# Four output buffers in place of two for the first expert layer of a two-layer decoder kernel

## The chip, the core and the metric

The kernel runs on one core of a Trainium2 chip. The core has a matrix engine (PE, with its weight loads as PEld), a vector engine (DVE), a scalar engine (ACT), a general engine (POOL), a sequencer that mostly issues DMAs (SP), and 16 DMA engines. Each engine works through its own instruction list in order, and they meet by semaphores. The metric is the device time of one launch in microseconds (us); lower is better.

## The reference

2048 tokens of 256 numbers go through two decoder layers. What matters here is the mixture of experts that closes the first layer:

```
scores = softmax(xt @ Wg.T)                      # 16 experts in 4 groups
gidx   = top_k(max of each group, 2)             # 2 groups kept
topi   = top_k(scores in the kept groups, 4)     # 4 experts for each token
h      = silu(xt @ W1[e]) * (xt @ W3[e])         # 176 wide, for each expert e
y      = sum over the 4 of score * (h @ W2[e])
z      = silu(xt @ Ws1.T) * (xt @ Ws3.T) @ Ws2.T # the shared experts
x      = layernorm(x + y + z)
```

Ahead of it stand a quadratic linear attention and a cross attention, behind it the second layer: a causal attention, a cross attention and a second mixture (8 experts, 2 for each token, 1024 wide).

## The kernel before

The stage in question is `moe0`. Tokens are sorted by expert into 79 slots of 128 rows (`NT`); a slot belongs to one expert. POOL scatters the token rows from SBUF into the table `xs` in HBM (L1614, an indirect DMA for each token tile and choice, 64 in all). The slots are then worked off in an order that a small table gives: SP (and ACT for the first seven) loads slot j's rows into `XG` once all the token tiles that the slot needs are in place. The result of a slot goes to the table `ys` in HBM, and POOL gathers it from there for each token tile (L1434, four indirect DMAs a tile), scales it by the gates and adds it to `X`.

The work on slot j is a software pipeline over four engines (`tile_pipeline`, L1411: a hardware loop with four slots a pass, the last seven slots written out). In step j:

- PE turns slot j+3 (`rows`, L1812), multiplies slot j+2 by W1 and W3 (`gate_up`, L1820), turns the product of slot j+1 (L1826), and multiplies slot j by W2 into the PSUM bank `BY[j % 2]` (L1840, L1842);
- ACT copies the turned rows j+3 (`XGT`, L1677), computes silu for slot j+2 (L1681), copies the turned product j+1 (L1685), and then issues the store of output j (`store`, L1688 to L1691), for which it waits until DVE has copied that output;
- DVE multiplies the gate of slot j+2 (L1756), and then copies output j from PSUM to `Y[j % 2]` in SBUF (L1764). This copy waits for `y_full` (PE is done with slot j) and for `stored[j % 2]` (the store of slot j-2, which read the same half of `Y`, has landed). It increments `y_used`.

So a copy to `Y` implies that the store of two slots before has landed. That is how POOL knows what it may gather: `ready_on_dve` (L1217) computes for each token tile t the place of the last slot that holds one of its rows, plus 1, plus `ahead` = 2, and POOL waits for `y_used` to reach it (`may_fetch`, L1627). At the end SP waits for all stores and adds 2 to `y_used` (L1580 to L1582), so that the last tiles can be released.

POOL's work in this stage is one chain: scatter, then for 12 of the 16 token tiles wait, gather, scale, add (`add_rows`, L1444). Two points in it are waited for by DVE: after tile 3 a semaphore `whole`, for which DVE waits behind slot 55 (moments of the first four tiles, L1482), and behind tile 9 the reciprocal roots of these moments (L1491, L1492), for which DVE waits behind slot 67 before it normalizes these tiles (L1497). Both sit in DVE's list between two hardware loops, ahead of the next slot's work.

PE ends the stage with ten matmuls whose results nobody reads (L152). A barrier of all engines follows, and then the second layer.

The second mixture, `moe1` (L2840 on), has the same pattern with its own `Y` of two buffers, ACT as the copying engine (L2994, L2995) and two semaphores `stored` of its own.

Of the kernel before, what the change touches and what calls it, by code (L numbers as in the profile page):

```python
# [14 lines left out]
BATCH, SEQ, DIM = 32, 64, 256  # L15
# [15 lines left out]
EPS_LN, EPS_RMS = 1e-5, 1e-6  # L31
NEG = -1.0e30
HS, SC = SHARED * I0, 3


REGION = TILES
# [1463 lines left out]
def moe0(nc, es, io, fx):  # L1500
# [8 lines left out]
    with ExitStack() as mem:  # L1509
# [3 lines left out]
        def sem(name):  # L1513
            return es.enter_context(nc.semaphore("m0_" + name))
# [7 lines left out]
        Z = sb("Z", [P, TILES, DIM])  # L1522
        XG, XGT = GS[:].rearrange("p a (b d) -> p (a b) d", d=DIM), sb("XGT", [P, 2, KC * P])
        SG, H, HT = sb("SG", [P, 2, I0]), sb("H", [P, 2, I0]), fx.HT
        Y = US[:, 0, :].rearrange("p (b d) -> p b d", d=DIM)
        BT, BH, BU, BY = fx.PJ, fx.SB[0:2], fx.SB[2:4], fx.OB
        ld_sh, ld_w, padded = fx.ld_sh, sem("ld_w"), fx.padded
        sh_full, sh_used, sh_h = sem("sh_full"), sem("sh_used"), sem("sh_h")
# [5 lines left out]
        u_full, gate, h_done = sem("u_full"), sem("gate"), sem("h_done")  # L1534
        ht_full, ht_used = sem("ht_full"), sem("ht_used")
        y_full, y_used = sem("y_full"), sem("y_used")
        stored = [sem(f"stored{b}") for b in range(2)]
        due, gathered = sem("due"), [sem(f"gathered{b}") for b in range(2)]

        with nc.Block() as block:  # L1540
            @block.sync
            def _(sp):
                for b in range(2):
                    sp.sem_inc(stored[b], 16)
                sp.wait_ge(fx.slots_zeroed, 64)
                for m in range(KC):
                    sp.dma_start(W13[:, m], io["w13"][m, :, 0:E0, :]).then_inc(ld_w, 16)
                sp.dma_start(W2A[:], io["w2"][0:P, 0:E0, :]).then_inc(ld_w, 16)
                sp.dma_start(W2B[0:KI], io["w2"][P:I0, 0:E0, :]).then_inc(ld_w, 16)
                sp.dma_start(W2B[KI:P], fx.zeros[KI:P].unsqueeze(1).broadcast_to([P - KI, E0, DIM])).then_inc(ld_w, 16)  # L1550
                sp.wait_ge(r.placed, 2)

                def load(j, b, checked=None):
                    if checked is not None:
                        need = sp.value_load(r.tneed[0:1, bass.ds(checked, 1)], min_val=1, max_val=TILES)
                    s = sp.value_load(r.tslot[0:1, bass.ds(j, 1)], min_val=0, max_val=NT - 1)
                    sp.wait_ge(t_full, j + 1)
                    if checked is not None:
                        sp.wait_ge(in_place, need)
                    sp.dma_start(XG[:, b, :].unsqueeze(1), slots[:, bass.ds(s, 1), :]).then_inc(ld_x[b], 16)  # L1560

                def weights():
                    fx.l1.load_weights(sp, io)

                load(FIRST, FIRST % 4, FIRST)
                with sp.Fori(0, CHECKED // 4) as i:
                    for b in range(4):
                        load(i * 4 + (FIRST + 1 + b), b, i * 4 + (FIRST + 4) if b == 0 else None)
                sp.wait_ge(in_place, TILES)
                done = FIRST + 1 + CHECKED  # L1570
                for upto, visit in ((48, weights), (NT - (NT - done) % 4, None)):
                    with sp.Fori(0, (upto - done) // 4) as i:
                        for b in range(4):
                            load(i * 4 + (done + b), b)
                    if visit:
                        visit()
                    done = upto
                for j in range(NT - (NT - FIRST - 1) % 4, NT):
                    load(j, j % 4)
                for b in range(2):  # L1580
                    sp.wait_ge(stored[b], 16 + 16 * ((NT + 1 - b) // 2))
                sp.sem_inc(y_used, 2)  # L1582

            @block.gpsimd
            def _(pool):
# [39 lines left out]
                own = fx.pool_steps  # L1625

                def may_fetch(t):  # L1627
                    pool.wait_ge(y_used, pool.value_load(r.ready[0:1, t:t + 1], min_val=3, max_val=NT + 2))
                    pool.sem_inc(due, 1)

                def fetch(t, k):
# [17 lines left out]
            def _(act):  # L1649
# [38 lines left out]
                def store(j, b):  # L1688
                    s = act.value_load(r.tslot[0:1, bass.ds(j, 1)], min_val=0, max_val=NT - 1)
                    act.wait_ge(y_used, j + 1)  # L1690
                    act.dma_start(rows_out[:, bass.ds(s, 1), :], Y[:, b % 2, :].unsqueeze(1)).then_inc(stored[b % 2], 16)  # L1691

                def step(j, b, ahead):
                    if follows(ahead, 3):
# [35 lines left out]
            def _(dve):  # L1730
# [10 lines left out]
                def gated(n):  # L1741
# [5 lines left out]

                r.order_on_dve(nc, dve, fx.slot_no[:], fx.ident[:], fx.tile_row[:], BU[0], BU[1], gated,
                               ((POOL_GATES, POOL_GATES + 1), (POOL_GATES + 2,)))
                r.ready_on_dve(nc, dve, fx.ident[:], BU[0], BU[1], 2, gated,  # L1750
                               ((POOL_GATES + 3,), (POOL_GATES + 4,)))
                gated(POOL_GATES + 5)

# [5 lines left out]
                def step(j, b, ahead):  # L1759
                    if follows(ahead, 2):  # L1760
                        product(j + 2, b + 2)
                    dve.wait_ge(y_full, j + 1)
                    dve.wait_ge(stored[b % 2], 8 * (j + (2 - b % 2)))
                    nc.vector.tensor_copy(Y[:, b % 2, :], BY[b % 2][:, 0:DIM]).then_inc(y_used, 1)  # L1764

                product(0, 0)
                product(1, 1)
# [1047 lines left out]
def moe1(nc, es, io, fx):  # L2815
# [7 lines left out]
    with ExitStack() as mem:  # L2823
# [3 lines left out]
        def sem(name):  # L2827
            return es.enter_context(nc.semaphore("m1_" + name))
# [24 lines left out]
        t_full, t_used = sem("t_full"), sem("t_used")  # L2853
        u_full, h_gelu = sem("u_full"), sem("h_gelu")
        y_full, y_used, finished = sem("y_full"), sem("y_used"), sem("finished")
        stored = [sem(f"stored{b}") for b in range(2)]
        due, gathered = sem("due"), [sem(f"gathered{i}") for i in range(AHEAD)]
        moments, root = sem("moments"), sem("root")
        normed, written = sem("normed"), sem("written")
# [5 lines left out]
        with nc.Block() as block:  # L2865
            @block.sync
            def _(sp):
# [29 lines left out]
                def step(j, b, ahead, checked=False):  # L2897
                    if follows(ahead, 6):
                        load(j + 6, (b + 2) % 4, checked)
                    if follows(ahead, WB):  # L2900
                        load_w1(j + WB, b, 2 * j + 4)
                    s = slot(j)
                    sp.wait_ge(stored[(b + 1) % 2], 8 * j + (16 if b % 2 == 0 else 24))
                    sp.sem_inc(finished, 1)  # L2904
                    sp.wait_ge(y_used, j + 1)
                    sp.dma_start(rows_out[:, bass.ds(s, 1), :], Y[:, b % 2, :].unsqueeze(1)).then_inc(stored[b % 2], 16)

# [7 lines left out]
                sp.wait_ge(in_place, TILES)  # L2915
                tile_pipeline(sp, step, NS, done=CHECKED)
                for b in range(2):
                    sp.wait_ge(stored[b], 16 + 16 * ((NS + 1 - b) // 2))
                sp.sem_inc(finished, 1)
                sp.wait_ge(written, 16 * POOL_WRITES)  # L2920
                sp.wait_ge(ld_s, 48 + 16 * (PAIRS - POOL_WRITES))
# [52 lines left out]
            def _(act):  # L2974
# [13 lines left out]
                def step(j, b, ahead):  # L2988
                    if follows(ahead, 2):
                        rows(j + 2, b)  # L2990
                    if follows(ahead, 1):
                        gelu(j + 1, b + 1)
                    act.wait_ge(y_full, j + 1)
                    act.wait_ge(stored[b % 2], 8 * (j + (2 - b % 2)))  # L2994
                    nc.scalar.activation(Y[:, b % 2, :], BY[b % 2][:, 0:DIM], ACT.Copy).then_inc(y_used, 1)  # L2995

                act.sem_inc(t_used, FIRST)
# [192 lines left out]
def decoder(nc, io):  # L3190
    es = ExitStack()
    with es:
        fx = Fixed()

        def sb(name, shape):
# [25 lines left out]
        fx.slots_zeroed = es.enter_context(nc.semaphore("slots_zeroed"))  # L3221
        fx.LG1 = sb("LG1", [P, TILES, E1])
        fx.early_table = es.enter_context(nc.sbuf_tensor("early_table", [P, 2, EARLY_TILES], I32))
        fx.early_placed, fx.early_sent, fx.in_place = (es.enter_context(nc.semaphore(n)) for n in (
            "early_placed", "early_sent", "in_place"))
        early = es.enter_context(ExitStack())
# [103 lines left out]
```

## Time and profile before

| | us |
|---|---|
| median of three runs | 1193.8 |
| the three runs | 1188.15, 1193.8, 1194.08 |
| the profiled execution | 1193.7 |
| its span, first to last instruction | 1191.9 |
| share of the span: PE, DVE, ACT, POOL | 91%, 42%, 42%, 37% |
| granted PE clock, mean | 0.964 |

The profiled execution lies 0.1 us from the median. 1.8 us of its time lie outside the span. All positions in the text are microseconds from the start of the span. The stage `moe0` runs its expert loop from about 384 to 616 us; the second mixture's loop takes the last 300 us. "m_US" in rows of `moe0` is the tile that `Y` is a part of, "m_GS" the one that `XG` is a part of, "bank" is PSUM, "inputs" is the tile that holds `HT`. PE works in float32 here, with several passes for one product, so a row of L1820 counts x4 for one slot.

### The profile page before, as it was taken

The numbers are of one execution on the slowest core, as the hardware profiler recorded it, in microseconds if no ns is written. First come the engines' busy times: TensorE is split into PE (matmuls) and PEld (weight loads), VectorE is DVE, ScalarE is ACT, GpSimd is POOL, SyncE is SP. The second block draws the span as 40 slices with busy tenths as digits, with TensorE's granted clock in tenths as the row PEclk, the third lists the DMA queues.
The fourth block names the chain that finished last, engine by engine and source line by source line (L and its number), as shares of the span: only waits on it lengthen the run. The fifth ranks groups of instructions, "written<-read, shape, count | busy, mean of one in ns | idle before, by whom it ended". The sixth has DMA issues, their size and how long they took to land. (4 is left out here: it accounts for less than half of the span.)

```text
span 1191.9 us, 29025 instructions
## 1 busy us (share of the span) xinstructions
PE 1087.6 (91%) x10260; PEld 838.5 (70%) x10261; DVE 496.3 (42%) x1340; ACT 504.1 (42%) x1306; POOL 439.9 (37%) x563
## 2 busy tenths in 40 slices
PE   8889989988898679999988999998789999999998
PEld 4466666655455347777756777786579899899997
DVE  2366665545571113333325666767443800000323
ACT  2444544444432123333334666575344333333333
POOL 2022131311248852777654666332524000200434
PEclk9999999999999669999999999999789999999999
DMA  6199478021283334565536111000157555555673
GB/s 202 45 311 362 161 237 268 21 81 55 118 258 118 129 113 126 154 191 150 144 120 284 37 37 53 22 19 3 56 194 237 187 175 177 174 175 174 194 240 107
DMA packets 119339, 176.09 MB, mean 148 GB/s; under 512 B 17440, under 2 KB 96912, under 8 KB 117776
## 3 DMA queue, kind: packets, MB, share of 16 engines
q1 hardware_dynamic: 94448, 135.55, 34.9%
q0 software_dynamic: 9696, 26.75, 6.9%
q10 hardware_dynamic: 15088, 12.28, 3.1%
q8 instruction: 77, 1.26, 0.4%
q14 instruction: 30, 0.25, 0.1%
HBM read 105.07 MB, written 68.16 MB: 145 GB/s over the span
## 5 line engine op out<-in xcount | busy, mean ns | idle before, releaser
L3149 PE MATMUL bank<-w,m_HT 128*128 x624 | 141.0, 379 | 0.0
L2984 ACT ACTIVATE m_HT<-bank,m_b 128x128 f32<-128x128 f32 x312 | 88.9, 370 | 90.2 <-PE bank L3135 74.2
L3149 PEld LDWEIGHTS bank<-w,m_HT 128*128 128x128 f32 x624 | 115.7, 190 | 14.1
L1820 PE MATMUL bank<-m_W,m_XGT 128*128 x316 | 114.0, 485 | 9.0 <-ACT m_XGT L1677 6.8
L1434 POOL DMA_INDIRECT GA<-ys,r_pos x64 | 64.7, 1010 | 62.9 <-DVE m_US L1764 43.0
L1677 ACT ACTIVATE m_XGT<-bank 128x256 f32<-128x256 f32 x79 | 30.3, 384 | 129.2 <-DVE m_US L1764 80.1
L1756 DVE TENSOR_TENSOR m_H<-bank,m_SG 128x176 f32<-128x176 f32 x79 | 26.9, 341 | 135.7 <-ACT m_SG L1681 96.9
L2948 POOL DMA_INDIRECT m_GA<-ys,r_pos x32 | 31.6, 986 | 133.6 <-SPq L2904 124.9
L3135 PE MATMUL bank<-m_XGT,m_w1a 128*128 128x128 f32 x640 | 77.3, 279 | 2.6 <-issue 1.8
L1820 PEld LDWEIGHTS bank<-m_W,m_XGT 128*128 128x128 f32 x316 | 56.6, 199 | 30.2 <-issue 14.3
L3135 PEld LDWEIGHTS bank<-m_XGT,m_w1a 128*128 128x128 f32 x640 | 75.0, 195 | 3.5 <-issue 2.3
L1614 POOL DMA_INDIRECT xs<-X,r_pos x64 | 63.2, 987 | 27.8 <-issue 14.6
L3135 PE MATMUL bank<-m_XGT,m_w 128*128 128x128 f32 x608 | 71.0, 275 | 0.0
L3135 PEld LDWEIGHTS bank<-m_XGT,m_w 128*128 128x128 f32 x608 | 69.5, 192 | 0.1
L405 POOL TENSOR_SCALAR l_rs<-l_mv 128x2 f32<-128x2 f32 x16 | 3.6, 225 | 158.2 <-DVE l_mv L669 157.9
L1764 DVE COPY m_US<-bank 128x256 f32<-128x256 f32 x79 | 33.5, 424 | 48.8 <-PE bank L1842 32.5
L1840 PE MATMUL bank<-m_W2A,inputs 128*128 x158 | 50.9, 405 | 2.9 <-issue 1.8
L1842 PE MATMUL bank<-m_W2B,inputs 128*128 x158 | 49.3, 395 | 0.0
L2995 ACT ACTIVATE m_Y<-bank 128x256 f32<-128x256 f32 x39 | 15.1, 386 | 80.2 <-PE bank L3149 75.5
L64 PE MATMUL bank<-XT,inputs 128*128 128x512 f32 x96 | 43.2, 596 | 2.7 <-ACT raw L481 1.3
L3057 DVE TENSOR_TENSOR X<-bank,X 128x512 f32<-128x512 f32 x8 | 5.5, 692 | 94.0 <-PE bank L3111 94.0
L2553 PE MATMUL bank<-l_VX,l_WX 128*64 128x54 f32 x1024 | 37.8, 234 | 7.5 <-issue 5.6
(475 smaller groups left out, 2301.3 us busy)
## 6 DMA issues: line engine op xcount, KB each, us to landing
m_w1a<-in_m_w SPq DMA_DIRECT2D x20, 1024.0 KB
m_w<-in_m_w SPq DMA_DIRECT2D x19, 1024.0 KB
xs<-zeros SPq DMA_DIRECT2D x1, 10112.0 KB, 34.2
ys<-zeros SPq DMA_DIRECT2D x1, 10112.0 KB, 34.6
ys<-m_US ACTq DMA_DIRECT2D x79, 128.0 KB
m_GS<-xs SPq DMA_DIRECT2D x72, 128.0 KB
w<-in_m_w SPq DMA_DIRECT2D x8, 1024.0 KB, 11.9
xs<-zeros SPq DMA_DIRECT2D x1, 6400.0 KB, 23.7
```

The lines of the kernel that those rows point to most:

```text
L64: last = nc.tensor.matmul(dst, stills[i], movings[i], start=i == 0, stop=i == n - 1)
L1434: pool.indirect_dma_start(out=fx.GA[:, t % 2 * (t < EARLY), k, :], out_offset=None, in_=fx.ys, in_offset=bass.IndirectOffsetOnAxis(ap=fx.p ...
L1614: pool.indirect_dma_start(out=fx.xs, out_offset=bass.IndirectOffsetOnAxis(ap=r.pos[:, t, k:k + 1], axis=0), in_=fx.X[:, t, :], in_offset=N ...
L1764: nc.vector.tensor_copy(Y[:, b % 2, :], BY[b % 2][:, 0:DIM]).then_inc(y_used, 1)
L1820: last = nc.tensor.matmul(BU[b % 2][:, 0:IW], XGT[:, b % 2, m * P:(m + 1) * P], W13[:, m, bass.ds(e, 1), :], start=m == 0, stop=m == KC - 1)
L1840: nc.tensor.matmul(BY[b % 2][:, 0:DIM], HT[:, b % 2, 0, :], W2A[:, bass.ds(e, 1), :], start=True, stop=False)
L1842: nc.tensor.matmul(BY[b % 2][:, 0:DIM], HT[:, b % 2, 1, :], W2B[:, bass.ds(e, 1), :], start=False, stop=True).then_inc(y_full, 1)
L2553: last = nc.tensor.matmul(repeated(OB[t][a * SEQ:(a + 1) * SEQ, n * 18:(n + 3) * 18], 18), WX[:, t, r, m, c], over_again(VX[:, j % 2, t, h ...
L2948: pool.indirect_dma_start(out=GA[:, t, k, :], out_offset=None, in_=fx.ys, in_offset=bass.IndirectOffsetOnAxis(ap=fx.pos1[:, t, k:k + 1], a ...
L2984: last = nc.scalar.activation(HT[:, b % 2, at, :], BU[i][:, c * P:(c + 1) * P], ACT.Gelu, bias=b1[:, b % WB, at:at + 1])
L3135: last = nc.tensor.matmul(BU[i][:, c * P:(c + 1) * P], w1[b][:, m, lo:lo + P], XGT[:, b % 2, m * P:(m + 1) * P], start=m == 0, stop=m == K ...
L3149: last = nc.tensor.matmul(BY[b % 2][:, 0:DIM], HT[:, b % 2, c, :], w2[:, bass.ds(e, 1), c, :], start=c == 0, stop=c == CH - 1)
```

## The change

`Y` gets four buffers: the whole tile `US` in place of its first half. Each buffer has its own store semaphore (`stored` with four entries, allocated for the whole kernel instead of for the stage). A copy to `Y[j % 4]` now waits for the store of slot j-4. What POOL may gather is released accordingly: `ahead` is 4, and the end adds 4 to `y_used`. The second mixture goes on counting on the first two of the same semaphores, so that its thresholds have an offset (`stores_of_first`).

```diff
+YB = 4
-        Y = US[:, 0, :].rearrange("p (b d) -> p b d", d=DIM)
+        Y = US[:].rearrange("p i (b d) -> p (i b) d", d=DIM)
-        stored = [sem(f"stored{b}") for b in range(2)]
+        stored = fx.stored
@@ moe0, SP
-                for b in range(2):
+                for b in range(YB):
                     sp.sem_inc(stored[b], 16)
...
-                for b in range(2):
-                    sp.wait_ge(stored[b], 16 + 16 * ((NT + 1 - b) // 2))
-                sp.sem_inc(y_used, 2)
+                for b in range(YB):
+                    sp.wait_ge(stored[b], fx.stores_of_first[b])
+                sp.sem_inc(y_used, YB)
@@ moe0, POOL: may_fetch
-                    pool.wait_ge(y_used, pool.value_load(r.ready[0:1, t:t + 1], min_val=3, max_val=NT + 2))
+                    pool.wait_ge(y_used, pool.value_load(r.ready[0:1, t:t + 1], min_val=YB + 1, max_val=NT + YB))
@@ moe0, ACT: store
-                    act.dma_start(rows_out[:, bass.ds(s, 1), :], Y[:, b % 2, :].unsqueeze(1)).then_inc(stored[b % 2], 16)
+                    act.dma_start(rows_out[:, bass.ds(s, 1), :], Y[:, b, :].unsqueeze(1)).then_inc(stored[b], 16)
@@ moe0, DVE
-                r.ready_on_dve(nc, dve, fx.ident[:], BU[0], BU[1], 2, gated,
+                r.ready_on_dve(nc, dve, fx.ident[:], BU[0], BU[1], YB, gated,
...
-                    dve.wait_ge(stored[b % 2], 8 * (j + (2 - b % 2)))
-                    nc.vector.tensor_copy(Y[:, b % 2, :], BY[b % 2][:, 0:DIM]).then_inc(y_used, 1)
+                    dve.wait_ge(stored[b], 4 * j + (16 - 4 * b))
+                    nc.vector.tensor_copy(Y[:, b, :], BY[b % 2][:, 0:DIM]).then_inc(y_used, 1)
@@ moe1, SP and ACT: the same waits, with what moe0 has counted added
-                    sp.wait_ge(stored[(b + 1) % 2], 8 * j + (16 if b % 2 == 0 else 24))
+                    sp.wait_ge(stored[(b + 1) % 2], 8 * j + (16 if b % 2 == 0 else 24) + earlier[(b + 1) % 2])
...
-                    act.wait_ge(stored[b % 2], 8 * (j + (2 - b % 2)))
+                    act.wait_ge(stored[b % 2], 8 * j + (8 * (2 - b % 2) + earlier[b % 2]))
@@ whole kernel
+        fx.stored = [es.enter_context(nc.semaphore(f"stored{b}")) for b in range(YB)]
+        fx.stores_of_first = [16 + 16 * ((fx.NS0 - b + YB - 1) // YB) for b in range(YB)]
```

No engine's arithmetic changes and nothing of it changes place. What changes in the lists is how a copy takes its two waits. On DVE, slots 1, 2 and 3 of a pass of the hardware loop in `moe0` (bank 7 and bank 6 hold the outputs, `m0_US` is `Y`, ISA stands for an instruction that only waits) are, before:

```order
L1756 TENSOR_TENSOR m0_H<-bank5,m0_SG 128x176 [waits m0_gate]
L1764 COPY m0_US<-bank7 128x256 [waits m0_stored1,m0_y_full]
L1755 REGISTER_ALU
L1756 TENSOR_TENSOR m0_H<-bank4,m0_SG 128x176 [waits m0_gate]
L1763 REGISTER_ALU [waits m0_y_full]
L1764 COPY m0_US<-bank6 128x256 [waits m0_stored0]
L1755 REGISTER_ALU
L1756 TENSOR_TENSOR m0_H<-bank5,m0_SG 128x176 [waits m0_gate]
L1764 COPY m0_US<-bank7 128x256 [waits m0_stored1,m0_y_full]
```

and now:

```order
L1757 TENSOR_TENSOR m0_H<-bank5,m0_SG 128x176 [waits m0_gate]
L1763 REGISTER_ALU
L1764 ISA [waits m0_y_full]
L1765 COPY m0_US<-bank7 128x256 [waits stored1]
L1756 REGISTER_ALU
L1757 TENSOR_TENSOR m0_H<-bank4,m0_SG 128x176 [waits m0_gate]
L1764 ISA [waits m0_y_full]
L1765 COPY m0_US<-bank6 128x256 [waits stored2]
L1756 REGISTER_ALU
L1757 TENSOR_TENSOR m0_H<-bank5,m0_SG 128x176 [waits m0_gate]
L1764 ISA [waits m0_y_full]
L1765 COPY m0_US<-bank7 128x256 [waits stored3]
```

Each copy now waits only for its own buffer's semaphore, and the wait for `y_full` stands in an instruction ahead of it; the copies of odd slots used to carry both waits themselves. A pass of four slots has three more sequencer instructions in each of DVE's two hardware loops; the slots written out behind them wait as before.

On ACT, in the second mixture's loop, the copy of an odd slot's output (`m1_Y` from bank 7) was:

```order
L2981 REGISTER_ALU
L2984 ACTIVATE m1_HT<-bank3,m1_b1 128x128 [waits m1_u_full]
L2984 ACTIVATE m1_HT<-bank3,m1_b1 128x128 x3
L2995 ACTIVATE m1_Y<-bank7 128x256 [waits m1_stored1,m1_y_full]
L2976 REGISTER_ALU
```

and is now:

```order
L2982 REGISTER_ALU
L2985 ACTIVATE m1_HT<-bank3,m1_b1 128x128 [waits m1_u_full]
L2985 ACTIVATE m1_HT<-bank3,m1_b1 128x128 x3
L2995 ISA [waits m1_y_full]
L2996 ACTIVATE m1_Y<-bank7 128x256 [waits stored1]
L2977 REGISTER_ALU
```

Here too the odd copy's wait for `m1_y_full` has moved into an instruction of its own.

## Rows read from the trace of the kernel before

**Rows 1.** Page, part 2: the clock of PE in 40 slices of 29.8 us, in tenths.

```profile
PEclk9999999999999669999999999999789999999999
```

**Rows 2.** Waits, 385 to 625 us: engine, its work <- releaser: us in total, times, longest.

```profile
POOL GA L1434 <- DVE m_US L1764: 43.0, 6, 27.3
DVE m_US L1764 <- PE bank L1842: 32.5, 56, 3.9
...
DVE m_US L1764 <- DMA ys<-m_US: 1.4, 1, 1.4
```

**Rows 3.** Timeline, one steady step: start, us, engine, line, op [idle before <-releaser].

```profile
447.63 0.42 DVE L1764 COPY m_US<-bank 128x256 f32<-128x256 f32 x1 [0.48 <-PE bank L1842]
...
448.21 0.34 ACTq L1691 DMA_DIRECT2D ys<-m_US  x1
...
448.67 0.38 ACT L1677 ACTIVATE m_XGT<-bank 128x256 f32<-128x256 f32 x1 [1.57 <-DVE m_US L1764]
...
450.03 0.42 DVE L1764 COPY m_US<-bank 128x256 f32<-128x256 f32 x1 [0.39 <-PE bank L1842]
450.05 0.46 PE L1820 MATMUL bank<-m_W,m_XGT 128*128 x1
```

**Rows 4.** Timeline, the stretch in which POOL still scatters.

```profile
388.33 0.59 PE L1842 MATMUL bank<-m_W2B,inputs 128*128 x2
...
391.84 0.42 DVE L1764 COPY m_US<-bank 128x256 f32<-128x256 f32 x1 [3.86 <-PE bank L1842]
...
399.77 0.42 DVE L1764 COPY m_US<-bank 128x256 f32<-128x256 f32 x1 [3.65 <-remote]
...
407.13 0.42 DVE L1764 COPY m_US<-bank 128x256 f32<-128x256 f32 x1 [2.33 <-remote]
```

**Rows 5.** Timeline, around the copy that waits for a store.

```profile
523.07 0.34 ACTq L1691 DMA_DIRECT2D ys<-m_US  x1
...
527.38 1.35 PE L1820 MATMUL bank<-m_W,m_XGT 128*128 x4
...
528.38 0.42 DVE L1764 COPY m_US<-bank 128x256 f32<-128x256 f32 x1 [1.40 <-DMA ys<-m_US]
...
529.94 1.45 PE L1820 MATMUL bank<-m_W,m_XGT 128*128 x4
...
532.70 1.45 PE L1820 MATMUL bank<-m_W,m_XGT 128*128 x4
```

**Rows 6.** Source line 1764 (the copy of an output), 391 to 498 and 391 to 503 us.

```profile
L1764 DVE COPY m_US<-bank x31: 424/425/426, 391.8 to 497.6; 128x256 f32<-128x256 f32 x31
...
L1764 DVE COPY m_US<-bank x33: 424/425/426, 391.8 to 502.6; 128x256 f32<-128x256 f32 x33
```

**Rows 7.** Timeline of POOL: gathers of tiles 3 and 11, and its last work here.

```profile
498.83 1.03 POOL L1434 DMA_INDIRECT GA<-ys,r_pos  x1 [5.00 <-DVE m_US L1764]
...
586.18 1.05 POOL L1492 TENSOR_TENSOR l_rs<-l_rs,neghalf 128x4 f32<-128x4 f32 x1
593.75 1.10 POOL L1434 DMA_INDIRECT GA<-ys,r_pos  x1 [6.53 <-DVE m_US L1764]
...
607.69 0.72 POOL L1454 TENSOR_TENSOR X<-X,GA 128x256 f32<-128x256 f32 x1
```

**Rows 8.** Timeline, DVE at the moments; DVE and PE at the normalization.

```profile
560.50 1.39 DVE L1482 BATCH_NORM_STATS2 l_st<-X 128x6 f32<-128x256 f32 x4
...
590.36 1.37 DVE L1497 TENSOR_SCALAR X<-X,l_mv,l_rs 128x256 f32<-128x256 f32 x4
...
591.92 0.34 DVE L1756 TENSOR_TENSOR m_H<-bank,m_SG 128x176 f32<-128x176 f32 x1 [0.19 <-ACT m_SG L1681]
...
593.71 0.27 PE L1826 MATMUL bank<-ident,m_H 128*128 128x128 f32 x1
...
595.01 1.35 PE L1820 MATMUL bank<-m_W,m_XGT 128*128 x4
```

**Rows 9.** Timeline, first work of POOL behind the stage.

```profile
619.52 1.91 POOL L2030 MEMSET l_VS<- 128x2176 f32 x1 [11.10 <-POOLq L1540]
```

More of the change, by code:

```diff
@@ L2855, in moe1 @@
         y_full, y_used, finished = sem("y_full"), sem("y_used"), sem("finished")
-        stored = [sem(f"stored{b}") for b in range(2)]
+        stored, earlier = fx.stored, fx.stores_of_first
         due, gathered = sem("due"), [sem(f"gathered{i}") for i in range(AHEAD)]
@@ L2917, in _ @@
                 for b in range(2):
-                    sp.wait_ge(stored[b], 16 + 16 * ((NS + 1 - b) // 2))
+                    sp.wait_ge(stored[b], earlier[b] + 16 + 16 * ((NS + 1 - b) // 2))
                 sp.sem_inc(finished, 1)
```

## The prediction

> **What bounds the kernel now.** I read first the waits of the stage that the change touches, because a double buffer is worth something only if somebody waits for it. In 385 to 625 us DVE waited once for a store, 1.4 us in all; behind PE it waited 56 times for 32.5 us [rows 2]. POOL waited 43.0 us for DVE's copies, that is for the release of the gathers [rows 2]. Then I read one steady step in the timeline. PE is the engine with no gap: from the 31st to the 33rd copy 5.0 us pass, 2.5 us a slot [rows 6], and at full clock in all slices there but two [rows 1]. The reader is to see in rows 3 how little of the copy's chain matters: copy at 447.63, store issued at 448.21, ACT's next rows at 448.67 to 449.05, and PE needs these rows at 450.05. So about 1.0 us of slack lies between DVE's copy and PE. A store has from its issue (0.58 us after its copy starts) to the copy two slots later, 5.0 - 0.6 = 4.4 us, to land, and in the steady step nobody waits for it.
>
> Two stretches are different. At 391 to 438 us, where the clock falls to half [rows 1], a slot takes 7 to 8 us: copies at 391.84, 399.77, 407.13 [rows 4]. And around 528 us one copy waits for a store [rows 5].
>
> **The change part by part.** The sum is made against the profiled execution: 1191.9 us span, 1193.7 us with what lies around it, 0.1 under the median.
>
> *The waits that go.* The copy at 528.38 waited 1.40 us, against 0.4 to 0.5 in a steady step, so it came 0.9 to 1.0 us late. It waited for the store issued at 523.07, which took some 5.3 us. PE felt little: its next products follow 2.56 and 2.76 us apart (527.38, 529.94, 532.70) in place of 2.5 [rows 5], 0.3 us in all. With four buffers the store has 9.4 us, and the wait is gone. Gain 0.3 us; its ends are 0 and the whole 1.4 us of wait.
>
> The Trainium skill ("DMA: Bandwidth & Descriptors", on the fixed cost of a DMA) puts about 2 us on every DMA, mostly the receipt of the write, and adds bytes over 436 GB/s. By that a 128 KB store is an estimated 2.3 us, two buffers with 4.4 us never wait, and the gain would be 0. The row at 528.38 disagrees with that for one store of 79; the same section of the Trainium skill also allows a "surprisingly long delay" for writes to HBM, which is this case.
>
> *The slow stretch, 391 to 438 us.* If its copies waited for stores, this would be the big term. I read that they don't. Copies 0 and 1 wait for no store, as their semaphores start at 16. Yet copy 0 starts 2.9 us after PE is done with its slot (388.92), and copy 1 comes 7.9 us after copy 0 with an idle time that ends on "remote", not on a DMA [rows 4]. Copy 2 needs the store of slot 0, issued near 392.4, and starts at 407.13, 14.7 us later; no store that the trace blames took over 5.3. So the term is 0.
>
> *The released gathers.* A copy now implies that the store of four slots before has landed, so POOL waits for two more copies. Tile 3's gathers were released by the 31st copy (the last one before 498.83 [rows 6, 7]) and now by the 33rd: 502.6 - 497.6 = 5.0 us later. Of POOL's six waits for DVE, 43.0 us in all, three are long: 27.3 for the first tile, 5.0 for tile 3 and 6.5 for tile 11 [rows 2, 7]. The others share 4.2 us, so tiles 4 to 10 follow POOL's own chain and all move by 5.0 us, and with them the roots behind tile 9: they end at 586.18 + 1.05 = 587.2 us, now 592.2. The moments have cover: tile 11 takes POOL 608.4 - 593.8 = 14.6 us from its first gather to its last addition; even at twice that, tile 3, started at 503.8, is added up by 533, and DVE wants it at 560.50 [rows 7, 8]. Cost 0.
>
> DVE reaches the normalization at 590.36 and needs those roots [rows 8]. Before, they were 3.1 us early; now they are 1.9 us late, and this is a new wait. Queued behind it on DVE are four normalizations (1.37 us), the gate product for PE's next turn, and the copy that lets ACT issue a store and then fetch rows. The product moves from 591.92 to 593.6 and ends at 593.9; PE wanted it at 593.71 [rows 8], so PE loses 0.3 us. The copy starts at 593.95, ACT's rows end 1.04 + 0.38 us behind a copy's start [rows 3], at 595.4, and PE starts on them at about 595.5 instead of 595.01 [rows 8]: 0.5 us lost in all, these 0.3 included. After that the slack of 1.0 us takes the rest. Ends: 0, and the whole 1.9 us.
>
> This stall is tied to POOL's clock, which hangs on the 33rd copy, and that lies ahead of the 0.3 us won at 528. Won time makes DVE arrive sooner and wait longer. So behind 595 us the 0.3 is swallowed and the stage stands at +0.5, not +0.2. I take +0.5.
>
> POOL's last work moves from 608.4 to 613.4, or by the release of tile 11 two copies later than 593.75 to the same. POOL's next work is at 619.52 [rows 7, 9]. 6.1 us of cover hide it; beyond that each us would cost one. The final wait for four semaphores instead of two waits for the same last store: 0.
>
> *The waits' new form.* An odd slot's copy starts 0.39 us, an even one's 0.48 us behind the product before it [rows 3]; now all have the even form, 0.09 us more for every second slot. In steady steps the 1.0 us of slack hides it. In the slow stretch copy, store and rows follow on each other, and three odd copies add 0.3 us (ends 0 and 0.3). In the second mixture ACT's odd copy gets the same 0.1 us. PE's chain there waits for no copy of an output, so it costs 0; without that cover, 19 odd slots would be 2 us.
>
> Sum: +0.5 + 0.3 = +0.8 us: span 1192.7, time 1194.5 us.
>
> **The rivals.** What can be told from no change here is about 0.5%, 6 us, so nearly everything above is "the same".
>
> *Faster: the stretch at 391 us is a wait for stores after all.* For it: it is where DMAs of POOL's scatter are in flight, and a copy's two waits can't be told apart if one is unrecorded. Against it: copies 0 and 1, as above [rows 4]. Then about six slots fall from 7.4 to 2.5 us: 6 x 4.9 = 29 us, 1165 us. If only one or two slots are freed, 5 to 10 us, 1184 to 1189.
>
> *Slower: the stretch at 391 us holds more slots.* Place: the loop of copy, store, rows, product and copy, which there runs once in 7.4 us. The new instruction ahead of an odd copy lies on it. If it makes the loop miss the end of the stretch by a slot, that slot costs 4.9 us more; from two slots on (9.8 us, 1204 us) it is over 0.5%. For it: the stretch is sensitive to something that no row names. Against it: 0.3 us in 46 is little.
>
> *Slower: code loading in DVE's loop.* Its two loops run 17 passes and get longer by three instructions. If a pass had to load its code again, it would stall as long as the worst idle times there, 3.9 us [rows 4], of which 1.0 us is covered: 17 x 2.9 = 49 us, 1243 us. No steady step shows such a stall [rows 3]. The Trainium skill ("Runtime: NRT & Kernel Launch", on instruction fetch) says that a taken branch out of the window of two pages forces a fetch; a loop of some 20 instructions would leave that window in no pass.
>
> *The change does nothing.* The released gathers are not the last thing POOL waits for, or the root is in time: then 1193.7 less 0.3, and the reader sees no idle time ahead of L1497's normalizations.
>
> **How the numbers follow.** Small terms only, within 0.5%: 0.81, the "does nothing" case included. Stretch freed: 0.08, of it most over 0.5%. Stretch longer: 0.06. Code loading: 0.02. Other shifts of an execution, such as the runs' own 1188 to 1194: 0.03, both ways. So faster by over 0.5% 0.09, the same 0.82, slower 0.09. Time 1194.5 us. The range takes in the ends of the terms (from -1.4 to +4.5), the spread of the three runs, and one slot won or lost in the stretch (4.9 us): 1188 to 1200.
>
> **What would show it.** The copy near 528 us has no wait on a DMA, and DVE shows none for a store in the whole stage. POOL's wait for tile 3 ends about 5 us later, at the 33rd copy. The normalization starts about 592 us with an idle time before it that POOL ended. POOL's last addition ends near 613 us. The stretch still holds seven copies 7 to 8 us apart. The prediction is wrong if that stretch gets shorter or longer by a slot or more, or if POOL's later work sets the end of the stage.

## The result and the profile after

The changed kernel takes 1196.4 us (median of 20 runs, 1191.5 to 1201.9), the kernel before 1190.5 us (20 runs, 1182.4 to 1194.1). The ratio is 1.0055, 95% interval 1.0038 to 1.0072, that is 6.5 us (4.5 to 8.6) slower. The forecast was 1194.5 us and +0.8 us. The time lies in the range, but on the slow side of it: the ratio is just beyond the 0.5% that I had called "the same", a case to which I had given 0.09. That 1194.5 comes within 2 us of 1196.4 is luck in part: the three runs that I started from had a median of 1193.8 us, 3.3 us above that of the twenty, and this made up for more than half of the loss that the sum lacks. All ratios here leave out disturbed executions (a low clock over the whole run), which were one of e4's (1814.7 us) and one of the kernel before's on the chip of e7 to e10 (1215.0 us).

The profiled execution took 1199.9 us, its span is 1198.0 us. The waits of the stage are now:

```profile
POOL GA L1435 <- DVE m_US L1765: 43.4, 6, 24.9
DVE m_US L1765 <- PE bank L1843: 29.7, 52, 3.0
...
POOL l_VS L2031 <- POOLq L1541: 9.7, 1, 9.7
...
DVE l_par L2287 <- PEq L1541: 7.7, 1, 7.7
...
DVE X L1498 <- POOL l_rs L1493: 2.1, 1, 2.1
```

The wait for a store [rows 2] is gone. New are DVE's wait for POOL's roots (L1498, 2.1 us, forecast 1.9), and DVE waits 7.7 us at the barrier, where it waited 4.1 before:

```profile
DVE l_par L2286 <- PEq L1540: 4.1, 1, 4.1
```

POOL's timeline (start, duration, work, idle time before it and its releaser), tile 3, the roots, tile 11, the last addition, and the next layer:

```profile
498.05 1.03 POOL L1435 DMA_INDIRECT GA<-ys,r_pos  x1 [6.63 <-DVE m_US L1765]
...
585.39 1.04 POOL L1493 TENSOR_TENSOR l_rs<-l_rs,neghalf 128x4 f32<-128x4 f32 x1
594.15 1.10 POOL L1435 DMA_INDIRECT GA<-ys,r_pos  x1 [7.71 <-DVE m_US L1765]
...
608.09 0.73 POOL L1455 TENSOR_TENSOR X<-X,GA 128x256 f32<-128x256 f32 x1
618.50 1.91 POOL L2031 MEMSET l_VS<- 128x2176 f32 x1 [9.68 <-POOLq L1541]
```

Beside [rows 7] tile 3 and tile 11 seem hardly to have moved (498.83 and 593.75 before). But the loop runs 6 to 7 us ahead of the loop before here: copy 30 is at 491.8, before at 497.6. Counted in copies, tile 3 is now released by copy 32 instead of 30 (from 0), tile 11 by copy 70 instead of 68. The loop's lead comes from the stretch at 391 us, whose copies 0 and 6 were at 391.84 and 437.69 and are now at

```profile
389.99 0.42 DVE L1765 COPY m_US<-bank 128x256 f32<-128x256 f32 x1 [2.15 <-PE bank L1843]
...
421.36 0.42 DVE L1765 COPY m_US<-bank 128x256 f32<-128x256 f32 x1 [2.27 <-remote]
```

This lead is not the change's: the changed kernel profiled once more (e9 below) has copy 6 at 439.7, and three kernels with the two buffers of before (e12, e13, e14) have it at 418.6, 419.2 and 417.5. At copy 10 7.3 us of the lead are left. The lead is lost again before the second layer. The last dummy matmul ends 4.6 us earlier than before (614.67 against 619.25), POOL's first work in the second layer comes only 1.0 us earlier (618.50 against 619.52 [rows 9]).

So positions from the span's start tell little here. What can be compared is the way between two events of the program, from copy 10 (the slow stretch is over) to copy 67 (the last one ahead of the normalization), and from there to POOL's first work in the second layer (L2030, after L2031):

| kernel | ratio, 95% interval | copy 10 to 67 | 67 to layer 2 | both, less before |
|---|---|---|---|---|
| before | 1 | 142.4 | 29.5 | 0 |
| changed | 1.0055, 1.0038 to 1.0072 | 143.6 | 34.6 | +6.3 |
| e1 | 1.0061, 1.0039 to 1.0082 | 143.4 | 34.8 | +6.3 |
| e2 | 1.0009, 0.9991 to 1.0027 | 142.3 | 29.4 | -0.2 |
| e4 | 1.0002, 0.9985 to 1.0019 | 142.2 | 29.5 | -0.2 |
| e5 | 1.0057, 1.0037 to 1.0077 | 143.7 | 31.8 | +3.6 |
| e7 | 1.0016, 0.9998 to 1.0034 | 142.3 | 30.3 | +0.7 |
| e8 | 1.0039, 1.0021 to 1.0057 | 143.7 | 33.2 | +5.0 |
| e9 | 1.0052, 1.0032 to 1.0071 | 143.7 | 34.3 | +6.1 |
| e10 | 1.0122, 1.0098 to 1.0145 | 142.2 | 46.3 | +16.6 |
| e11 | 1.0015, 0.9990 to 1.0041 | 143.6 | 29.4 | +1.1 |
| e12 | 1.0019, 0.9988 to 1.0051 | 143.0 | 28.5 | -0.4 |
| e13 | 1.0024, 0.9996 to 1.0053 | 142.5 | 30.6 | +1.2 |
| e14 | 1.0000, 0.9978 to 1.0022 | 143.7 | 29.5 | +1.4 |

Each column of us is from one profile of that kernel. The 6.5 us of the ratio are found almost whole in these two stretches: 1.2 us in the loop and 5.1 us behind copy 67.

The spans of two profiles alone would not have shown this. From POOL's first work in the second layer to the end the profile of before has 572.4 us, the changed kernel's 579.5, e9's 574.7, and e2 and e4, whose times are those of before, have 576.1 and 577.3. In the pair of before and changed a lead of 7.3 us at copy 10 and a second layer 7.2 us longer happen to cancel, and the difference of the spans, 6.1 us, looks right by accident.

### The profile page after: what moved, and what is told of

It reads as the page before. It is cut to its first block and busy times, and to the rows that moved or that the text cites. A ratio compares the mean times of both kernels' runs of the same rounds, so it can differ in the third digit from the quotient of the medians.

```text
span 1198.0 us, 29045 instructions
## 1 busy us (share of the span) xinstructions
PE 1090.3 (91%) x10260; PEld 842.2 (70%) x10261; DVE 495.3 (41%) x1340; ACT 504.6 (42%) x1306; POOL 440.5 (37%) x563
## 3 DMA queue, kind: packets, MB, share of 16 engines
q1 hardware_dynamic: 94448, 135.55, 34.8%
## 5 line engine op out<-in xcount | busy, mean ns | idle before, releaser
L1821 PE MATMUL bank<-m_W,m_XGT 128*128 x316 | 111.1, 475 | 11.1 <-ACT m_XGT L1678 10.9
L1841 PE MATMUL bank<-m_W2A,inputs 128*128 x158 | 49.1, 393 | 4.1 <-issue 2.1
## 6 DMA issues: line engine op xcount, KB each, us to landing
ys<-zeros SPq DMA_DIRECT2D x1, 10112.0 KB, 34.3
```

The source lines that it names most:

```text
L1821: last = nc.tensor.matmul(BU[b % 2][:, 0:IW], XGT[:, b % 2, m * P:(m + 1) * P], W13[:, m, bass.ds(e, 1), :], start=m == 0, stop=m == KC - 1)
L1841: nc.tensor.matmul(BY[b % 2][:, 0:DIM], HT[:, b % 2, 0, :], W2A[:, bass.ds(e, 1), :], start=True, stop=False)
```

## The experiments

All ratios are against the kernel before on the same chip, from five rounds.

**e1, only the release later.** The kernel before, with

```diff
-                sp.sem_inc(y_used, 2)
+                sp.sem_inc(y_used, 4)
-    ... pool.value_load(r.ready[0:1, t:t + 1], min_val=3, max_val=NT + 2)
+    ... pool.value_load(r.ready[0:1, t:t + 1], min_val=5, max_val=NT + 4)
-                r.ready_on_dve(..., BU[0], BU[1], 2, gated,
+                r.ready_on_dve(..., BU[0], BU[1], 4, gated,
```

> The kernel before with two buffers, but with the release of the gathers two copies later (ahead = 4, and 4 added at the end), as the change has it. Medians of twenty runs each were 1190.5 us before and 1196.4 us after the change, so about 6 us are to be explained. Theory (POOL ends the stage): the release alone does it. POOL's last addition and the 9.2 us that it takes to drain behind it move by some 3 to 5 us, the barrier with them, PE idles longer ahead of the second layer and starts it at half clock: 1.003 to 1.006 of before, 1194.5 to 1198 us. Rival (second mixture: offsets and the new form of ACT's wait): 1.000. Rival (first mixture: DVE's own wait instruction and four store semaphores): 1.000.

Measured 1.0061, a hair above the 1.003 to 1.006. The release alone makes the whole loss; what the forecast says of the clock is taken up further down and does not hold. POOL's roots, tile 11, last addition and next work in e1, and DVE's normalization:

```profile
590.76 1.05 POOL L1492 TENSOR_TENSOR l_rs<-l_rs,neghalf 128x4 f32<-128x4 f32 x1
599.53 1.10 POOL L1434 DMA_INDIRECT GA<-ys,r_pos  x1 [7.72 <-DVE m_US L1764]
...
613.49 0.73 POOL L1454 TENSOR_TENSOR X<-X,GA 128x256 f32<-128x256 f32 x1
623.89 1.91 POOL L2030 MEMSET l_VS<- 128x2176 f32 x1 [9.68 <-POOLq L1540]
```

```profile
591.84 1.38 DVE L1497 TENSOR_SCALAR X<-X,l_mv,l_rs 128x256 f32<-128x256 f32 x4 [2.30 <-POOL l_rs L1492]
```

The reader is to see the last row of POOL: 9.68 us idle before L2030, where [rows 9] has 11.10. In all six profiles in which POOL is late (changed, e1, e8, e9, e10, e13) this idle time is 9.68 or 9.7 us. It is what POOL needs from its last addition to be through the stage's end: a drain, an instruction of its sequencer that stands at the end of the block, takes 9.22 us of it. The drains of before at the barrier (duration in ns, then start):

```profile
L1540 POOLq DRAIN  x1: 9222/9222/9222, 608.6 to 608.6; - x1
L1540 PEldq DRAIN  x1: 5213/5213/5213, 614.1 to 614.1; - x1
...
L1540 SPq DRAIN  x1: 7/7/7, 618.0 to 618.0; - x1
```

POOL's ended at 617.84, PE's last dummy at 619.25. The cover was 11.10 - 9.68 = 1.4 us, not 6.1.

**e2, four buffers, release as before.** The changed kernel, where a copy waits for the store of two slots before and `ahead` is 2:

```diff
-                    dve.wait_ge(stored[b], 4 * j + (16 - 4 * b))
+                    dve.wait_ge(stored[(b + 2) % YB], 4 * j + (16 if b < 2 else 32) - 4 * b)
```

> The changed kernel with its four buffers, but a copy waits for the store of two slots before, and the gathers are released as early as before (ahead = 2). Theory (POOL ends the stage): back to the time before, 0.998 to 1.001 of it, 1188 to 1192 us. Both rivals (second mixture's waits; first mixture's new form of waits and semaphores): it stays at the changed kernel's 1.005, about 1196 us, since those parts of the change are still in.

Measured 1.0009, and POOL's row is back at 11.10:

```profile
595.67 1.10 POOL L1435 DMA_INDIRECT GA<-ys,r_pos  x1 [6.48 <-DVE m_US L1765]
...
621.44 1.91 POOL L2031 MEMSET l_VS<- 128x2176 f32 x1 [11.10 <-POOLq L1541]
```

Buffers, semaphores, DVE's own wait instruction and the second mixture's offsets are all in e2, and cost nothing that can be measured.

**e4, only the second mixture.** The kernel before; the first mixture counts its two buffers on semaphores that the second goes on with, and only there the thresholds get their offsets:

```diff
-                    act.wait_ge(stored[b % 2], 8 * (j + (2 - b % 2)))
+                    act.wait_ge(stored[b % 2], 8 * j + (8 * (2 - b % 2) + earlier[b % 2]))
```

> The kernel before, with only the second mixture changed: it counts on semaphores that the first mixture has used, with the offsets in its thresholds, and so takes ACT's odd wait in an instruction of its own. Theory (POOL ends the first mixture's stage): 1.000, within 1.5 us of before. Rival (second mixture's waits): the whole loss, 1.005, 1196 us. Rival (first mixture's new form of waits): 1.000.

Measured 1.0002: nothing, as forecast. Its converse, the first mixture alone with four semaphores of its own, was not measured; e2 holds both parts.

**e10 and e13, the dose.** As e1, with 6 and with 3 in place of 4 for `ahead`.

> The kernel before with two buffers, and the release four copies later (ahead = 6) instead of two. Theory: POOL's roots come 10 us later, so the stall at the normalization is 6.7 to 7 us; POOL's end moves by 10 us and by the stall, less 1.4 us of cover: 15 us lost, 1.013 of before (1.011 to 1.015). Rival (what the first two copies cost is a fixed price, such as another clock at the start of the second layer): 1.006. Rival (each copy costs its 2.5 us alone, less the cover, and the stall does not reach POOL): 1.007.

> The kernel before with two buffers, and the release one copy later (ahead = 3). Theory (two covers, 3.1 us ahead of the normalization and 1.4 us behind POOL's drain): POOL's roots come 2.5 us later and are still in time, so no stall; POOL's end moves by 2.5 us, 1.1 us of it beyond the cover: 1.0009, and 30.6 us from copy 67 to the second layer's first work on POOL instead of 29.5. Rival (each copy costs the same, half of what two cost): 1.003, 32.1 us.

Measured 1.0122, and 1.0024 with an interval that holds both theories. The profile tells e13 apart: 30.6 us behind copy 67, as forecast to the tenth. Waits behind 560 us, e10 first:

```profile
POOL l_VS L2030 <- POOLq L1540: 9.7, 1, 9.7
...
DVE X L1497 <- POOL l_rs L1492: 6.8, 1, 6.8
```

```profile
POOL l_VS L2030 <- POOLq L1540: 9.7, 1, 9.7
...
DVE l_par L2286 <- PEq L1540: 5.2, 1, 5.2
```

Behind copy 67 one copy later costs 1.1 us, two 4.8 to 5.3, four 16.8: this fits a threshold at each of the two covers. In e10 the stall at the normalization is 6.8 us, and tile 11, which waits for a copy behind it, gets it on top of its four copies. The forecast's sum (10 + 6.8 - 1.4 = 15.4 us) is 1.4 us short of the 16.8: the loop is 8.3 us late at copy 70, not 6.8. The rival without the stall in POOL's end, 1.007, lies outside the interval.

**e8, the normalization later.** The changed kernel, with DVE's visit at slot 72 (and, in `tile_pipeline`, the hardware loop that this leaves empty skipped):

```diff
-                              (68, lambda: fx.l1.apply_on_dve(nc, dve, fx.X))))
+                              (72, lambda: fx.l1.apply_on_dve(nc, dve, fx.X))))
```

> The changed kernel, but DVE normalizes the first four token tiles behind slot 71 instead of slot 67, so that POOL's late roots are there. The theory so far: POOL's end of the stage is late by two copies (5.0 us) and by the stall of 1.5 to 1.8 us at the normalization, which lies ahead of copy 70 that releases tile 11; of the 6.7 us 1.4 are covered by PE's own end, and 5.3 are lost. Without the stall 3.6 us are left: 1.003 of the kernel before, 1.8 us less than the changed kernel on the same chip. Copy 68 then follows copy 67 by 2.5 us instead of 4.1. Rival (the stall delays only DVE and PE, and POOL's end hangs on its own chain alone): the same time as the changed kernel, 1.0055. Rival (the stall is the main cost): 1.000 to 1.001.

Measured 1.0039. The ratio alone does not part it from the changed kernel's 1.0052 (e9, same chip); the profile does: DVE does not wait for POOL, copy 68 follows copy 67 by 2.5 us, and POOL waits for tile 11 6.52 us instead of 7.71:

```profile
598.45 1.10 POOL L1437 DMA_INDIRECT GA<-ys,r_pos  x1 [6.52 <-DVE m_US L1767]
...
622.97 1.91 POOL L2033 MEMSET l_VS<- 128x2176 f32 x1 [9.68 <-POOLq L1543]
```

33.2 us behind copy 67 are 1.0 less than e9 has there, and 3.7 more than before, where 3.6 were forecast. The stall does reach POOL.

**e9, the changed kernel again.**

> The changed kernel once more, on the chip of these runs and with a profile. Theory (late release, POOL's 9.2 us of draining): 1.0055 of before, loss of 5.3 us in the stage; the stretch around 391 to 438 us is of the usual length this time, so that POOL's last drain ends near 623 us and the barrier with it, and not at 618 us as in the first profile. Rival (the changed kernel always has the shorter stretch, and loses more behind the stage): copy 6 is again at about 421 us and the second layer again longer by 8 us or more.

Measured 1.0052, without the short stretch, and the second layer is 2.3 us longer than before's, not 8 or more. POOL's drain ends at 628.4, 5.4 us behind the forecast: this execution was 3.0 us late at copy 10 already, the 1.3 us of the loop were not in the sum, and the drain itself moves by the whole lateness (6.2 us behind copy 67), from which I had taken off the cover.

```profile
POOL l_VS L2031 <- POOLq L1541: 9.7, 1, 9.7
...
DVE X L1498 <- POOL l_rs L1493: 1.8, 1, 1.8
```

**e5, e7 and e11, one tile less for POOL.** `EARLY = 11` in place of 12: in the changed kernel, in the kernel before, and in e8.

> The changed kernel, with POOL gathering and adding 11 token tiles in the first mixture's stage instead of 12; the twelfth is done in the first round of the second layer, like the other four. It takes about 14 us of POOL's work away from the end of the stage and adds them to the next. Theory (POOL ends the stage): the barrier is set by PE again, some 3.6 us earlier, PE's idle time is short enough that it stays at full clock, and the time goes to 0.993 to 1.001 of the kernel before (1182 to 1192 us), unless the second layer's first rounds pay for POOL's extra tile; then up to 1.006. Both rivals: no effect of the end of the stage, 1.005, 1196 us.

> The kernel before, with POOL gathering and adding 11 token tiles in the first mixture's stage, and the twelfth in the second layer's first round. The changed kernel with the same edit stayed at 1.0057, although its barrier was set by PE again. Theory: the extra tile costs the second layer 3 to 4 us, since POOL is waited for there, so this kernel is at 1.003 of before, and the changed one had 1.7 to 2.3 us of stall on top. Rival (the extra tile is free): 1.000, and then the changed kernel with 11 tiles loses its 6 us at something not yet named.

> The changed kernel with both escapes: the normalization behind slot 71 and eleven token tiles in the first mixture's stage. POOL then ends some 13 us ahead of PE and nobody waits for its roots. Theory: what is left is the price of the extra tile in the second layer alone, as the kernel before with eleven tiles had it, 1.0016 (1.000 to 1.003); from copy 67 to the second layer 29.5 us pass, as in the kernel before. Rival (a part of the loss, some 2.5 us, lies neither in the stall nor in POOL's end, since the changed kernel with eleven tiles had 1.0057 against 1.0016): 1.004.

e5 missed: 1.0057 instead of 0.993 to 1.001. I had expected the loss to go with POOL's end. The clause "then up to 1.006" had left room for it, and the rivals say 1.005, so its time alone decides nothing. e7 was forecast at 1.003, its rival at 1.000; 1.0016, with both inside its interval, decides nothing either. The profile of e5 says more: POOL is out of the way in it, and DVE waits at the barrier 4.1 us as in the kernel before; the stall at the normalization stays:

```profile
DVE l_par L2287 <- PEq L1541: 4.1, 1, 4.1
...
DVE X L1498 <- POOL l_rs L1493: 2.5, 1, 2.5
```

Its 3.6 us are 1.3 in the loop and 2.3 behind copy 67. The extra tile costs the second layer too: of e7's 1.9 us (its ratio) 0.7 lie in the two stretches (between copies 67 and 68, at no wait for POOL; I did not follow it), so 1.2 us behind them. This is an estimate, as e7's interval reaches from -0.2 to +4.1 us. For e5 that makes 4.8 us, 1.004, inside its interval near the lower end; for e11 1.1 + 1.2 = 2.3 us, 1.0019, measured 1.0015. So e5's escape took away 2.8 us behind copy 67 (34.6 to 31.8), not 6. e11, with both escapes, is back at 29.4 us there, as forecast, but the interval of its time reaches to the rival's 1.004.

**e12, six dummy matmuls in place of ten.** `busy(nc, BH[0], fx.ones[:], 3)` in the kernel before.

> The kernel before, with six instead of ten dummy matmuls at the end of the stage, whose results nobody reads in either kernel. They end 1.7 us earlier. Theory (PE sets the barrier before the change, POOL's drain is 1.4 us behind it): the barrier comes 1.4 us earlier, POOL's drain then sets it: 28.1 us from copy 67 to the second layer instead of 29.5; time 0.999, unless PE's longer idle time costs clock at the start of the second layer. Rival (POOL's drain sets the barrier already before the change, or it ends only when PE has ended): 29.5 us, unchanged.

The barrier came 1.0 us earlier, not 1.4:

```profile
POOL l_VS L2030 <- POOLq L1540: 10.1, 1, 10.1
```

The idle time is 10.12, not 9.68: POOL was through at 608.81, SP, which waits for the last stores, at 609.27. Thus three engines stood within 1.5 us of each other before the change. Dummies did set the end by a little; the time, 1.0019, shows no gain.

**e14, the first tile alone later.** What was left were 1.2 us in the loop. All six profiles with `ahead` = 4 lose them at one place, copy 21. Rows of e1 (gathers of the first tile, and DVE's copies 20 and 21):

```profile
469.32 0.99 POOL L1434 DMA_INDIRECT GA<-ys,r_pos  x1 [31.58 <-DVE m_US L1764]
...
470.59 0.42 DVE L1764 COPY m_US<-bank 128x256 f32<-128x256 f32 x1 [0.34 <-issue]
...
473.13 0.95 POOL L1434 DMA_INDIRECT GA<-ys,r_pos  x1 [0.30 <-issue]
...
475.12 0.42 DVE L1764 COPY m_US<-bank 128x256 f32<-128x256 f32 x1 [2.51 <-remote]
```

Copy 21 starts 4.5 us after copy 20. The first tile's four gathers follow each other at 1.25 to 1.30 us, and in them SP's own instructions get longer (the load of a register 0.70 instead of 0.27 us). The kernel before has the same two copies earlier, and there it costs next to nothing: SP's instructions get as long, copy 20 comes 3.0 us after copy 19, and copy 21 only 2.2 us behind it. The kernel before, with one line more:

```diff
                 may_fetch(0)
+                pool.wait_ge(y_used, 20)
```

> The kernel before, with one more wait on POOL: the gathers of the first token tile alone start when copy 19 is done instead of copy 17, as they do in the changed kernel. Tile 3 and all behind it are released as before. In all six kernels profiled so far with the release two copies later, copy 21 comes 4.5 to 4.7 us after copy 20, in the others 2.2 to 2.4 us, and copies 10 to 67 take 143.4 to 143.7 us instead of 142.2 to 142.4 (one of 143.0). Theory (the place of POOL's first four gathers in the loop costs this): copy 21 again 4.5 to 4.7 us after copy 20, 143.5 us from copy 10 to copy 67, POOL's wait for tile 3 shrinks from 5.0 us to about 0 to 1, from copy 67 to the second layer still 29.5 us: 1.3 us lost in all, 1.0011 of before. Rival (the delay comes from the later release as a whole, or from something else that differs): copy 21 2.2 to 2.5 us after copy 20, 142.3 us, 1.000.

The place is confirmed, the size in part: copy 21 comes 3.9 us after copy 20 (4.5 to 4.7 were forecast), 143.7 us from copy 10 to 67, and behind that 29.5. Of the 1.4 us that the loop is longer than before's only 0.9 lie between copies 18 and 24, where the late release costs 1.5 to 1.7; another 0.3 lie ahead of copy 18, next to the slow stretch. POOL's first gathers of tile 0 and of tile 3:

```profile
460.60 0.99 POOL L1434 DMA_INDIRECT GA<-ys,r_pos  x1 [22.58 <-DVE m_US L1765]
...
489.85 1.04 POOL L1434 DMA_INDIRECT GA<-ys,r_pos  x1 [1.37 <-DVE m_US L1765]
```

POOL's wait for tile 3 shrank from 5.00 to 1.37 us, so that tile and all behind it were not late. A time difference can't be seen (1.0000, interval to 1.0022, which holds the 1.0011). With `ahead` = 6 the same burst, two copies later still, costs nothing (142.2 us); so the 1.2 us hang on where the burst meets the loop, and are not a price of lateness. That it acts through SP's slower instructions is likely, but no run shows it. Why copy 21 suffers and copies 19, 20 or 23 hardly do, I can't say.

## Why the prediction was right and wrong

The time is in the range, the mechanism is only half right. The prediction named two signs of being wrong, and both came: POOL's later work does set the end of the stage, and the slow stretch was shorter in the first profile. The first is the failed step below, the second was chance. That a loss of 6.5 us still fits the range comes from the range's width: it had been made up of the ends of other terms, the runs' spread and a slot won or lost in the slow stretch, and held nothing for POOL's end. (The upper ends of the terms as I named them add up to 1.9 + 0.3 + 2 = 4.2 us, not 4.5.)

*The wait for a store.* Gone, as forecast, and worth what I took: copies 41 to 45 took 10.4 us before and take 9.95 us now, 0.4 us (forecast 0.3). The wait is no accident: eight of the nine profiled kernels in which a copy waits for the store two slots before show it, at copy 42 (e13 at 43), 0.5 to 2.0 us long, and from copy 41 to 45 these kernels take 9.9 to 10.9 us. Three of them (e2, e4, e12) wait for a store at copy 77 as well, 1.7 to 1.8 us, with nothing lost behind it: 28.5 to 29.5 us from copy 67 to the second layer.

*The slow stretch.* Term 0 confirmed: with four buffers (e9) it has its usual length, 48.0 us from copy 0 to 6 (before 45.8). The 31.4 us of the changed kernel's first profile have nothing to do with stores, as e12, e13 and e14 with two buffers have 30.1 to 32.0. Neither rival on that stretch, nor the one on code loading, shows in any profile.

*The roots.* Late by 2.1 us, forecast 1.9. The step "0.5 us lost in all, these 0.3 included. After that the slack of 1.0 us takes the rest" was mis-sized: copy 68 follows copy 67 by 4.1 us instead of 2.5, 1.6 us. The changed kernel at that place:

```profile
583.90 0.42 DVE L1765 COPY m_US<-bank 128x256 f32<-128x256 f32 x1 [0.48 <-PE bank L1843]
...
586.31 1.35 PE L1821 MATMUL bank<-m_W,m_XGT 128*128 x4
586.47 1.38 DVE L1498 TENSOR_SCALAR X<-X,l_mv,l_rs 128x256 f32<-128x256 f32 x4 [2.15 <-POOL l_rs L1493]
587.77 0.33 DVE L1757 TENSOR_TENSOR m_H<-bank,m_SG 128x176 f32<-128x176 f32 x1
588.02 0.41 DVE L1765 COPY m_US<-bank 128x256 f32<-128x256 f32 x1
...
588.16 0.33 PE L1827 MATMUL bank<-ident,m_H 128*128 128x128 f32 x1 [0.50 <-DVE m_H L1757]
...
589.02 0.69 PE L1841 MATMUL bank<-m_W2A,inputs 128*128 x2 [0.43 <-issue]
...
590.33 0.85 PE L1821 MATMUL bank<-m_W,m_XGT 128*128 x2
```

In [rows 8] PE's turn follows its product by 1.19 us (592.52 to 593.71 in the timeline), here by 1.85. Then 0.86 us pass to L1841, where 0.21 were usual. In them PE's sequencer loads and checks the expert's number for L1841 (L1808, 588.16 to 588.86); in the step of before it did so from 592.41 to 593.01, while the product still ran, and here only once the turn had started. The next product comes another 0.2 late. Together 1.5 us; I had priced the first at 0.3, not the second, and the third at 0.2.

*POOL's end: the step that failed.* I wrote "6.1 us of cover hide it; beyond that each us would cost one". The second half was right and the first wrong, twice. The idle time ahead of POOL's next work [rows 9] was released by POOLq, POOL's own sequencer; 9.7 of its 11.1 us were POOL's own ending, not cover: 1.4 us were left where I had counted 6.1. And tile 11 is released by copy 70, behind the stall, so POOL's end moved by two copies (5.0 us) and by the stall (1.6), not by 5.0: 5.0 + 1.6 - 1.4 = 5.2 us, measured 5.1. The term was 0 in my sum. The Trainium skill ("Perfetto Trace Analysis", on the GPSIMD engine instruction) says to treat a span of that engine as unreliable. No run here tests the spans themselves; what the traces show is that POOL's last vector record ends 9.4 us before its drain does (608.82 and 618.24 in the changed kernel).

*The waits' new form, and the second mixture.* Forecast 0.3 and 0; e2 and e4 show 0 within about 3 us (their intervals end at 1.0027 and 1.0019), and e2's loop has the same length as before's (142.3 and 142.4 us). The 0.3 us were put into the slow stretch, which varies by more than that, so they can't be seen.

*Not foreseen:* the collision at copy 21: copies 18 to 24 took 15.13 us before and take 16.67 now, 1.5 us more. Less the 0.4 of the store this makes 1.1 of the loop's 1.2 us.

*A story that was at hand and that the other profiles do not bear out.* The changed kernel's PE idles 5.9 us ahead of the second layer (before 2.4) and starts it at a granted clock of 0.55, near the lower level of 1.2 GHz, the kernel before at 1.00. So the idle time seems to cost clock, and the forecast of e1 says so. PE there (stretch, its length, busy time, granted clock, DMA share, GB/s), of before, of the changed kernel and of e2:

```profile
621.60:627.00 5.40, 4.18 (x20) 1.00 0.96 349
```

```profile
620.60:628.50 7.90, 7.16 (x20) 0.55 1.01 358
```

```profile
623.50:631.30 7.80, 7.02 (x20) 0.57 1.00 367
```

e2 idles as briefly ahead of it as the kernel before does (2.4 us) and has the low clock as well, as e4 has (0.59). From the first turn to the start of the 16th product behind it PE takes 5.2 us in the profiles of before and of e14 and 6.8 to 8.0 us in the twelve others, with the release of before or the later one; e2 and e4, with 2.4 us idle, have 7.6 and 8.0. So the fast start is a matter of the execution, and the longer idle time is not needed for the slow one. Seven profiles have 2.4 us idle there and two of them are fast; none of the seven with more is, and that is too few to rule out a small effect.

## What to carry to other kernels

More buffers are not free where a counter of "written" is derived from the buffers' reuse: with two more buffers every consumer of that counter is released two steps later (e1 alone gives the whole loss, e2 takes it away with the buffers still there). Before idle time is counted as cover, look at what ended it: if it is the engine's own sequencer, most of it may be work that the profile does not count as busy. And a lateness upstream has to be carried along every release behind it, stalls that it makes included, before it is compared with the cover.

## What the runs showed of the hardware that I had not expected

- POOL's drain behind its last vector work took 9.22 us in all eleven profiles with twelve tiles in the stage, and 8.90 in all three with eleven, however long POOL had still to wait; at three other ends of blocks of this kernel it took 0.8, 3.2 and 5.3 us.
- The stretch in which POOL scatters can differ by 16 us from one execution or chip to another, in the same kernel too (copy 6 at 417.5 to 439.7 us over all profiles; copies 0 to 6 in 31.4 and 48.0 us in the two profiles of the changed kernel).
- While POOL issued four indirect DMAs 1.25 to 1.30 us apart, the loop of the other engines came up to 2.2 us late at one copy, 1.5 to 1.7 us of it for good, depending on the slot that they met, and repeatably so (4.5 to 4.7 us between two copies in six profiles).
